# Two expert weights loaded during attention, one expert tile fewer, and a last stage shared with ScalarE

## The reference, cut to what matters

```python
x = x + attention(x)                # causal; scores = q.k + lam * (q_cos.k_cos + q_sin.k_sin)
x = layernorm(x)
gating = softmax(x @ Wg + bg)       # [.., 8]
top = argsort(gating)[..., -2:]     # two experts a token
h = silu((x @ W1[e] + b1[e]) * (x @ W3[e] + b3[e]))
y = h @ W2[e] + b2[e]
mixed = sum(gating[top] * y[top])
x = layernorm(x + mixed @ Wf + bf)
```

## Time and profile before

| | us |
|---|---|
| three timed runs | 2060.68, 2063.33, 2069.52 |
| median | 2063.33 |
| the profiled execution | 2052.71, its span 2051.1 |
| attention, by the profile | 237.5 to 1330.7 |
| routing | 1330.7 to 1526.4 |
| experts | 1526.4 to 1969.7 |
| last stage | 1969.7 to 2051.1 |
| root of one chunk on ScalarE (L1031) | 0.30 |
| one load of an activation table on ScalarE | 1.28, once in the last stage |

### The profile page before, as it was taken

The page is one execution under the profiler, slowest core; times in us unless marked ns, Lnnn a source line. Parts: engine busy times, 40 slices in busy tenths (PEclk is TensorE's granted clock), DMA queues, the critical chain, the costliest instruction groups (busy, mean ns, idle before and its releaser), DMA issues. The chain is left out here.

```text
span 2051.1 us, 28577 instructions
## 1 busy us (share of the span) xinstructions
PE 1738.7 (85%) x9152; PEld 918.5 (45%) x9153; DVE 1302.5 (64%) x3135; ACT 838.4 (41%) x941; POOL 366.9 (18%) x488
## 2 busy tenths in 40 slices
PE   6999179999999999999999999644429999999954
PEld 3444034444444444444444444134315666666643
DVE  3687577777777777777777775036625555555548
ACT  2677423455555555555555555402202221222211
POOL 0111111121121211112111121103553111111111
PEclk9999568899999999999999999867659999999978
DMA  3454421011020110201102000088521111111143
GB/s 97 144 205 174 176 101 44 7 47 54 7 99 7 54 51 4 99 7 63 43 11 90 7 13 12 11 254 251 201 91 34 46 46 46 46 42 46 44 130 132
DMA packets 99690, 155.57 MB, mean 76 GB/s; under 512 B 10784, under 2 KB 60896, under 8 KB 99200
## 3 DMA queue, kind: packets, MB, share of 16 engines
q1 hardware_dynamic: 85072, 122.66, 18.5%
q0 software_dynamic: 14512, 31.53, 4.3%
HBM read 88.04 MB, written 65.48 MB: 75 GB/s over the span
## 5 line engine op out<-in xcount | busy, mean ns | idle before, releaser
L862 ACT ACTIVATE att_probs<-att_ps_s 128x1024 f32<-128x1024 f32 (+3 forms) x640 | 563.9, 896 | 513.1 <-PE att_ps_s L817 505.8
L817 PE MATMUL att_ps_s<-att_queries,att_keys 49*128 49x512 f32 (+3 forms) x2560 | 628.8, 559 | 21.1 <-ACT att_probs L862 11.6
L876 DVE TENSOR_REDUCE att_maxima<-att_ps_m 128x1 f32<-128x512 f32 x768 | 487.1, 683 | 151.7 <-PE att_ps_m L796 146.6
L796 PE MATMUL att_ps_m<-att_keys,att_queries 48*128 48x512 f32 (+3 forms) x1280 | 502.4, 603 | 43.6 <-DMA att_keys<-k_parts 36.4
L796 PEld LDWEIGHTS att_ps_m<-att_keys,att_queries 48*128 48x128 f32 x1280 | 195.9, 192 | 336.0 <-DVE att_maxima L876 137.6
L879 DVE CUSTOM_DVE_ANT_0 att_ps_m<-att_ps_m,att_future 128x128 f32<-128x128 f32 (+3 forms) x512 | 240.2, 513 | 94.7 <-PE att_ps_m L796 93.4
L817 PEld LDWEIGHTS att_ps_s<-att_queries,att_keys 49*128 49x128 f32 x2560 | 240.2, 190 | 127.8 <-ACT att_probs L862 84.9
L838 PE MATMUL att_ps_o<-att_probs,att_values 128*32 128x512 f32 (+3 forms) x2560 | 269.4, 535 | 11.1 <-POOL att_probs L955 11.1
L1447 PE MATMUL exp_ps_h<-keep_w,exp_rows_t 128*128 x576 | 261.0, 596 | 5.5 <-DVE exp_rows_t L1478 5.5
L1520 ACT ACTIVATE exp_hidden<-exp_product 128x512 f32<-128x512 f32 x72 | 45.4, 631 | 324.8 <-DVE exp_product L1503 324.8
L955 POOL TENSOR_SCALAR_AFFINE_SELECT att_probs<-att_probs 128x512 f32<-128x512 f32 x128 | 81.5, 636 | 489.4 <-ACT att_probs L862 489.3
(11 more groups left out here) (188 smaller groups left out, 1482.4 us busy)
## 6 DMA issues: line engine op xcount, KB each, us to landing
att_queries<-q_parts SPq DMA_DIRECT2D x64, 192.0 KB
att_keys<-k_parts SPq DMA_DIRECT2D x64, 192.0 KB
exp_rows<-sorted_rows SPq DMA_DIRECT2D x72, 129.0 KB, 2.3
v_rows<-pre_v_sb SPq DMA_DIRECT2D x8, 1024.0 KB, 4.4
q_parts<-pre_waves SPq DMA_DIRECT2D x16, 512.0 KB, 3.0
k_parts<-pre_waves SPq DMA_DIRECT2D x16, 512.0 KB, 4.2
att_values<-v_rows SPq DMA_DIRECT2D x32, 256.0 KB, 14.7
out_parts<-att_out_t POOLq DMA_DIRECT2D x32, 256.0 KB, 5.9
```

Source lines behind the costliest of these rows:

```text
L796: pe.matmul(take()[:, 0:width], queries[half, g % 2, c, r, P * q:P * q + P], keys[half, g % 2, k, r, 0:width], start=True, stop=True).then ...
L817: mm = pe.matmul(score_tile(unit, first, last)[:, e], keys[half, g % 2, k // TPC, r, P * (k % TPC):P * (k % TPC) + P].bitcast(F32), querie ...
L862: act.activation(probs[:, step % PROBS, DUO * r:DUO * r + DUO, first:last], score_tile(unit, first, last), ACT.Exp, scale=SCALE).then_inc( ...
L876: dve.tensor_reduce(to, buf[:, 0:width], AX.X, ALU.max).then_inc(s_mr, 1)
```

## The change

Five things are changed together.

1. The weights W1 and W3 are allocated for the whole rest of the program and loaded by SyncE in attend, behind the loads of quad 1 (four transfers of 2048 KB). What route still issues are the four parts of W2 and the three biases, seven transfers, one with each chunk from 1 on.
2. Queries, keys and values of a chunk count on one semaphore, and TensorE waits for all of them before the chunk's first maxima. The wait for the values ahead of the products with them is gone.
3. The probabilities have 6 buffers, not 8.
4. There are 71 expert tiles.
5. In the last stage ScalarE weighs the first rows and normalises, as x * rstd + shift; VectorE makes shift = -mean * rstd. The residual has two buffers. The entries of the pipelines are ordered anew, and ScalarE's is now written out in full.

```diff
-SLOT_TILES = T * TOPK // P + NE
+SLOT_TILES = T * TOPK // P + NE - 1
-PROBS = 8
+PROBS = 6
...
-        s_q = [[n_.sem(f"q_loaded{i}_{c}") for c in range(QC)] for i in range(2)]
-        s_k = [[n_.sem(f"k_loaded{i}_{c}") for c in range(QC)] for i in range(2)]
-        s_v = [[n_.sem(f"v_loaded{i}_{c}") for c in range(QC)] for i in range(2)]
+        s_qkv = [[n_.sem(f"q_k_v_loaded{i}_{c}") for c in range(QC)] for i in range(2)]
+        s_expert = n_.sem("expert_weights_loaded")
+        LOADS = 16 * (2 * DUO + 1)
...
                 for c in range(QC):
-                    load(queries, rows_q, s_q, g, c)
-                    load(keys, rows_k, s_k, g, c)
+                    load(queries, rows_q, g, c)
+                    load(keys, rows_k, g, c)
                     load_v(g, c)
+                if g == 1:
+                    for to, rows in first_weights:
+                        sp.dma_start(to, rows).then_inc(s_expert, 16)
+            sp.wait_ge(s_expert, 16 * len(first_weights))
...
                 if (r, q, e) == (0, 0, 0):
-                    pe.wait_ge(s_q[g % 2][c], 32 * (g // 2 + 1))
-                    pe.wait_ge(s_k[g % 2][k], 32 * (g // 2 + 1))
+                    pe.wait_ge(s_qkv[g % 2][c], LOADS * (g // 2 + 1))
...
-                if k % TPC == 0:
-                    pe.wait_ge(s_v[g % 2][k // TPC], 16 * (g // 2 + 1))
...
+def weight_blocks(to, weight):
+
+    return [(to[:, k], weight[:, k * P:(k + 1) * P].rearrange("e p h -> p e h")) for k in range(to.shape[1])]
...
-            later = [(dst[:, k], src[:, k * P:(k + 1) * P].rearrange("e p h -> p e h"))
-                     for dst, src, tiles_k in ((w1, W1, DK), (w3, W3, DK), (w2, W2, HK)) for k in range(tiles_k)]
+            later = weight_blocks(w2, W2)
...
-        res = n.sb("res", [P, TPC, D])
+        res = n.sb("res", [P, 2, TPC, D])
+        shift = n.sb("shift", [P, TPC])
...
         @block.scalar
+            def weigh_first(i, p):
+                act.wait_ge(s_pick[p], 16 * TOPK * ((i >> 1) + 1))
+                if since(i, 2):
+                    act.wait_ge(s_mp, i - 1)
+                for t in range(TPC):
+                    act.activation(mixed[:, p, t], picked[:, p, 0, t], ACT.Copy, scale=gate(0, i, t)).then_inc(s_first, 1)
+
+            def normalise(i, p):
+                act.wait_ge(s_shift, i + 1)
+                if since(i, 2):
+                    act.wait_ge(s_out[p], 16 * (i >> 1))
+                for t in range(TPC):
+                    act.activation(normed[:, p, t], res[:, p, t], ACT.Identity, scale=norm.rstd[:, t:t + 1],
+                                   bias=shift[:, t:t + 1]).then_inc(norm.s_done, 1)
...
-            pipelined(act, NCH, [(keep_mixed, 0), (lambda i, p: norm.root(act, i, eps[:, 0:1]), 2)])
+            pipelined(act, NCH, [(normalise, 4), (weigh_first, 0), (keep_mixed, 1), (lambda i, p: norm.root(act, i, eps[:, 0:1]), 3)])
...
         @block.vector
             def mix(i, p):
                 dve.wait_ge(s_pick[p], 16 * TOPK * ((i >> 1) + 1))
-                if since(i, 2):
-                    dve.wait_ge(s_mp, i - 1)
-                for t in range(TPC):
-                    dve.tensor_scalar(mixed[:, p, t], picked[:, p, 0, t], gate(0, t), None, ALU.mult).then_inc(s_first, 1)
                 for t in range(TPC):
                     dve.wait_ge(s_first, i * TPC + (t + 1))
...
             def residual(i, p):
                 dve.wait_ge(s_y, i + 1)
-                if since(i, 1):
-                    dve.wait_ge(norm.s_done, i * TPC)
-                dve.tensor_tensor(res[:, :], ps_y[p][:, :], x1_chunk, ALU.add).then_inc(s_res, 1)
+                if since(i, 2):
+                    dve.wait_ge(norm.s_done, (i - 1) * TPC)
+                dve.tensor_tensor(res[:, p], ps_y[p][:, :], x1[:, i * TPC:i * TPC + TPC, 0:D], ALU.add).then_inc(s_res, 1)
                 dve.wait_ge(s_res, i + 1)
+                norm.statistics(dve, i, res[:, p], in_order=True)
+
+            def scale_and_shift(i, p):
+                dve.wait_ge(norm.s_std, i + 1)
+                dve.reciprocal(norm.rstd[:, :], norm.rstd[:, :]).then_inc(norm.s_rstd, 1)
+                dve.wait_ge(norm.s_rstd, i + 1)
+                if since(i, 1):
+                    dve.wait_ge(norm.s_done, i * TPC)
+                dve.scalar_tensor_tensor(shift[:, :], norm.mean, -1.0, norm.rstd[:, :], ALU.mult, ALU.mult).then_inc(s_shift, 1)
-            pipelined(dve, NCH, [(mix, 0), (normalise, 3), (residual, 2)])
+            pipelined(dve, NCH, [(mix, 0), (scale_and_shift, 3), (residual, 2)])
```

## The result

The changed kernel takes 2013.69 us (median of 4 runs, 2011.78 to 2014.97), the kernel before 2062.01 (4 runs, 2060.0 to 2069.52): a ratio of 0.9758, interval 0.9731 to 0.9785, so 48 us faster by the medians. Forecast were 2018 us and 2002 to 2037. The two profiled executions differ by less: 2052.71 to 2014.97, 37.7 us.

What follows compares the result with a forecast made beforehand. TensorE bounds attention and experts, transfers then an engine chain routing, VectorE the last stage. 29 - 4 + 5.8 + 14.3 = 45.1 us off the profiled 2052.71 gives 2007.6; adding the median's 10.6 offset gives 2018, range 2002 to 2037.

Steps and rivals of the forecast that it cites:

- Routing, ahead of the last divide: Routing, first to last divide: without W1 and W3 loads there, 25 us come back, between 18.7 and 29.
- Rival (a): Routing's first stretch: transfers themselves bind, not their order; routing gives only 15 us, result 2032; chance 0.17.
- Routing, the tail: Routing after the last divide: GpSimd's scatters, further behind, cover VectorE's waits without local releaser; 4 us gained, 0 to 13.
- Rival (c): Routing's tail closes up wholly: routing gives 42 us, result 2005; chance 0.08.
- Attention: Attention stage: 4 us lost to early loads and the shared semaphore, 0.5 to 20; growth under 6 us as sign.
- the maxima row: Attention near 330 us: chunk 2's maxima row lands later beside the W1 and W3 stream; 3 us lost, 0 to 18.
- the values: Start of attention, quad 0's chunks 0 and 1: TensorE awaits values before maxima; 1 us lost, 0 to 5.2.
- Rival (d): Attention: W1 and W3 stream to 403 us, TensorE stands 70 us for chunk 2's maxima row; result 2084; chance 0.04.
- Six buffers: Attention: neither 8 nor 6 probability buffers bind, so the order of work stays; cost 0.
- 71 tiles: Expert stage: one tile less at 5.82 us a tile gives 5.8 us; code fetches could cost 0 to 3.
- Last stage: Last stage: VectorE's period falls from 7.81 to 5.47 us with ScalarE at 4.4; 14.3 us gained.
- rival (b): Last stage: ScalarE binds at 7.3 us a period through table loads; stage gives 3 us, result 2030; chance 0.13.

Runs made afterwards that it cites:

- changed, again: The changed kernel measured again without any edit; 2021.14 us, ratio 0.9797 to the kernel before.
- early loads alone: Kernel before with W1 and W3 loaded in attention, six probability buffers, queries and keys on one semaphore, values on their own; 2037.34 us, ratio 0.9891.
- stream at quad 5: Changed kernel with W1 and W3 issued behind quad 5's loads instead of quad 1's; 2012.81 us (0.9774), measured a second time 2017.76 (0.9788).
- the repetitions: Changed kernel measured again, 2021.14 us (0.9797), and once more through a flag for written-out routing programs that changed nothing, 2018.54 us (0.9809).
- values apart: Changed kernel with the values on their own semaphore again, awaited only at their first product; 2019.15 us, ratio 0.9795 to the kernel before.

## Why the prediction was right, step by step

**Routing, ahead of the last divide: 25 us forecast, 27.2 measured.** The stalls behind W1 and W3 went, as named. Over the traces with early loads the first and last divide lie 86 to 96 us apart, over those without 114 to 117; the means, 90.2 and 115.7, lie 25.5 apart. The named remainder is there too: before the last two divides 2.41 and 3.82 us are lost, one of them to a transfer. Rival (a), 15 us, falls. The engines move 264 GB/s here at 0.78 busy, under the 275 that I had named: with compute as the bound of most chunks they idle at times. One bound of mine was worked out wrongly: seven intervals of 12.4 us, less the choice of 4.4 in two, are 78 us and not 85, so the most that could come back was 36 us, not 29, and 25 was a guess between other ends than I wrote. Intervals without a stall measured 10.2 to 11.6.

**Routing, the tail: 4 us forecast, 0 measured; this step failed.** I took it that GpSimd would be further behind when the tail begins, so that its scatters would cover the waits without a local releaser. It is not: at the last divide it waits for places (5.84 us, ahead of 1442.72) as it did before (11.16), 40 scatters follow it in both kernels, and the wait of 12.0 us stands ahead of the places that GpSimd waits for. Even without it only 4.66 us can come back, since from 1480.09 on the last 16 scatters at 1.27 us end the stage by themselves: places of chunk 6 are given only after the logits of chunk 7. Giving them earlier was not tried. Rival (c), 13 us more, was thus never open, and the stage came to 169 us, not to the 165 that I had named.

**Attention: 4 us lost forecast, 7.1 measured; this term was too small.** The two mechanisms were right in kind and size: 3 us for the maxima row, measured 3.2; 1 us for the values, measured 0.9 at their own place. But attention grew by more than the 6 us that I had named as a sign, and the group means below lie 9.6 us apart with the stream at quad 1 and 5.4 with it at quad 5. The row's landing nearly doubled (2.8 to 5.1 us), as assumed. By the Trainium skill (DMA: Bandwidth & Descriptors, Queues, rings and completion order) it would wait for single packets only; the 5.1 us beside a stream at 321 to 370 GB/s are on that side, far from the 18 of a common queue, but the cost was not near 0. Rival (d) falls: the stream ended near 350 us, and TensorE's two waits sum to 4.3. What I had left out of the sum is the clock. With W1 and W3 in attention its mean length is 1102.0 us at quad 1 (8 traces) and 1097.8 at quad 5 (2), against 1092.4 without (4). Adding up (1 - granted clock) over stretches of 10 us from 160 to 1020 us after its start gives a time by which the clock fell short:

| kernel | attention, us | clock short by, us |
|---|---|---|
| before | 1093.2 | 6.8 |
| 71 tiles | 1092.7 | 5.1 |
| six buffers | 1088.1 | 5.1 |
| changed | 1100.3 | 10.2 |
| changed, again | 1106.2 | 17.0 |
| early loads alone | 1096.7 | 6.8 |
| stream at quad 5 | 1098.9 | 11.9 |

Less that sum, the eight traces with the stream at quad 1 have a mean of 1090.3 and the six others 1086.6: 3.7 us, about the forecast. This takes every shortfall for lost time, which is an estimate: some short falls cost nothing (last section). Whether the change makes the clock fall more often, or these executions happened to, stays open: the early loads alone have no more of it than the kernel before.

**Six buffers: 0 forecast**, +2.9 us measured with an interval that holds 0, and its trace has the shortest attention (1088.1). **71 tiles: 5.8 forecast**; 5.9 in the profile, 6.8 by the part alone, 6.1 between the means of the stage. The results of VectorE in tiles 0 and 67, after, are 390.01 us apart, 5.82 a tile as before; the last tiles follow faster, when the stages ahead of them have run out of work:

```profile
1533.96 0.42 DVE L1515 TENSOR_TENSOR exp_result<-exp_ps_y,keep_bias 128x256 f32<-128x256 f32 x1 [0.21 <-PE exp_ps_y L1470]
...
1923.97 0.42 DVE L1515 TENSOR_TENSOR exp_result<-exp_ps_y,keep_bias 128x256 f32<-128x256 f32 x1 [0.22 <-PE exp_ps_y L1470]
```

**Last stage: 14.3 us forecast, 14.1 measured**, 14.4 by the part alone. VectorE's period came out at 5.35 to 5.6 against 5.47. ScalarE's share was 4.76 us instead of 4.4: normalising takes 0.50 us an operation (1.98 from the start of four to what follows), weighing 0.40 (1.59), where I had taken 0.38 from a read of PSUM. By the Trainium skill (ScalarE: Activation LUTs, Rules for kernel authors) an operation costs 0.51, an estimate worked out from its figures; for normalising the trace agrees, for weighing it is less. The conclusion drawn from it, a ScalarE that ties with VectorE, did not come: 4.76 is below 5.35. No table was reloaded, so rival (b) falls.

**The sum and the offset.** Forecast were 45.1 us off the profiled execution; the profile gives 37.8: routing 26.5, tiles 5.9, last stage 14.1, attention -7.1, the first stage -1.6. That is 7.3 less. The median came out right nevertheless, and by luck, because the offset of 10.6 us that I had added back was no property of the kernel: the profiled execution of before was one of its shorter ones (over all runs here it takes 2047.5 to 2069.5 us), and the changed kernel's profiled execution lies 1.3 above its own median. The sum thus fell 7.4 us too low (2007.6 against 2014.97), the offset 11.9 too high (+10.6 against -1.3), and the forecast 4.3 above the median. Two errors thus cancelled. Against the repetitions (2021.14 and 2018.54) the forecast lies 3.1 and 0.5 us on the other side; the spread of one kernel's executions is larger than any of these distances.

## What to carry to other kernels

When transfers crowd one stage, look for an earlier one with idle queues and a buffer that can live that long: 8.4 MB moved into attention gave routing 25 us. Attention grew by 5 to 10 us, of which two waits explain about 4; by the total of the kernel with the early loads alone, 22.4 us remained. What shares the queues there pays in small waits of the critical engine, and once behind them in its clock. Before crediting an experiment with an answer, check that its edit reaches the program: a flag that asks for straight code does nothing where the helper writes straight code already, and a loop does not hold the iteration that was in question. For a chain that is handed from engine to engine at the end of a stage, ask at which instruction a later resource takes over (here 16 scatters from 1480.09 us) before crediting it with any gain: that caps what covering a wait can bring.

## What the runs showed of the hardware

One kernel's executions on one chip spread over 15 us (2010.8 to 2026.18), and the clock goes with it: the two fastest of the five (2010.8 and 2014.03) have a mean granted clock of 0.927, the three others 0.923 to 0.924. The traces of all kernels show where in attention it falls. It does so, if it does, near 215, 345, 470, 600, 725 and 850 us after the start, some 127 us apart, where one quad's work passes into the next. The kernel before, and the one with values apart, at the same turn: TensorE's wait and then two stretches of 10 us.

```profile
450.30 0.42 PE L838 MATMUL att_ps_o<-att_probs,att_values 128*32 128x128 f32 x8 [1.03 <-POOL att_probs L955]
```
```profile
450.00:460.00 10.00, 9.70 (x60) 4.14 (x61) 7.49 (x17) 4.67 (x5) 3.13 (x6) 1.00 0.33 120
460.00:470.00 10.00, 9.83 (x64) 5.02 (x60) 8.60 (x20) 6.70 (x8) 1.09 (x2) 1.00 0.27 99
```
```profile
456.12 0.42 PE L842 MATMUL att_ps_o<-att_probs,att_values 128*32 128x128 f32 x8 [1.61 <-POOL att_probs L959]
```
```profile
450.00:460.00 10.00, 8.23 (x62) 4.21 (x55) 6.27 (x14) 3.13 (x5) 3.10 (x5) 0.90 0.33 111
460.00:470.00 10.00, 10.00 (x39) 4.05 (x38) 4.29 (x11) 3.24 (x4) 1.60 (x3) 0.58 0.24 91
```

In the one execution the clock stayed at full speed behind a wait of 1.03 us for GpSimd's masked probabilities; in the other a wait of 1.61 us was followed by a fall to half speed (the two levels are 2.4 and 1.2 GHz), and from the first reduction to the negated maxima behind it to the next took 53.5 us instead of 49.9. The same wait is 1.29 us in the changed kernel, with a short fall too, and the step took 50.5. Over all fourteen traces this step is 53.3 to 53.5 us in the five where the clock stood near its lower level for some 8 us, and 49.7 to 50.6 in the nine others, six of which had a short fall: a long fall cost about 3 us, a short one nothing that can be seen. A fall followed at 47 of the 84 passages (six in each trace). TensorE's wait for GpSimd there averages 1.77 us ahead of a fall and 1.24 where none came, and between 1.29 and 1.75 us both happened. In a kernel with such a place, single profiles differ by more than small edits are worth: compare the stage lengths over several.
